# Tile stages of a mixture-of-experts kernel: the first quad in two halves, the second handed over in two, and another order of gate and down products in the first eight quads

## What is computed

```
flat = x.reshape(B * T, D)
logits = flat @ router_w.T + router_bias
scores = softmax(logits); topk_scores, topk_idx = top_k(scores, 4)   # 32 experts
topk_scores = topk_scores / topk_scores.sum(-1)
h = silu(flat @ gate_w[e]) * (flat @ up_w[e]);  expert_out = h @ down_w[e]
out = sum over the 4 chosen experts of expert_out * topk_score
out = out + silu(flat @ sgate_w.T) * (flat @ sup_w.T) @ sdown_w.T     # shared part
```

## Time and profile before

| | us |
|---|---|
| three timed runs | 927.50, 923.75, 927.27 |
| their median | 927.27 |
| the profiled execution, its own time | 923.53 |
| its span (first to last instruction) | 922.3 |
| mean granted TensorE clock | 0.925 of full speed |
| first tile stage, first tile load issued to last POOL scatter issued | 497.15 to 632.87 |
| second tile stage, the same | 765.63 to 899.70 |
| busy in the whole span: PE 82%, PE weight load 67%, DVE 59%, POOL 54%, ACT 46% | |

### The profile page before, as it was taken

The page is one execution under the profiler, slowest core; times in us unless marked ns, Lnnn a source line. Parts: engine busy times, 40 slices in busy tenths (PEclk is TensorE's granted clock), DMA queues, the critical chain, the costliest instruction groups (busy, mean ns, idle before and its releaser), DMA issues.

```text
span 922.3 us, 18791 instructions
## 1 busy us (share of the span) xinstructions
PE 755.3 (82%) x6384; PEld 616.0 (67%) x6384; DVE 546.8 (59%) x1655; ACT 427.9 (46%) x1099; POOL 494.6 (54%) x488
## 2 busy tenths in 40 slices
PE   6899988889999998878998899915988997999600
PEld 5778755579967777767776788813666775888500
DVE  5974585668677758878873444401977662454205
ACT  3567646556145545555521666620454322666500
POOL 5555540016283024655673577776347772677773
PEclk9999979999889999999999999966998999999955
DMA  9999999900050041001112544314101113444216
GB/s 228 220 216 216 215 219 216 209 6 4 4 160 23 1 129 32 2 32 35 48 57 75 136 123 125 102 52 168 43 26 53 55 58 89 122 124 124 72 51 233
DMA packets 125757, 94.67 MB, mean 103 GB/s; under 512 B 10624, under 2 KB 116480, under 8 KB 125664
## 3 DMA queue, kind: packets, MB, share of 16 engines
q1 hardware_dynamic: 113472, 71.19, 33.7%
q0 software_dynamic: 10176, 21.65, 6.8%
q10 hardware_dynamic: 2016, 0.63, 0.3%
HBM read 34.05 MB, written 59.38 MB: 101 GB/s over the span
## 4 chain that ended last, share of the span: by engine, by line
PE 43%; DVE 19%; POOL 19%; issue 11%; ACT 4%; DMA 3%; SPq 0%; POOLq 0%; DVEq 0%; ACTq 0%
POOL expert_rows L677 10%; POOL sorted_rows L445 8%; PE banks L1638 5%; PE banks L1110 4%; PE banks L1685 3%; PE banks L1667 3%; PE banks L783 2%; PE banks L396 2%; PE banks L397 2%; PE banks L398 2%; DVE h L744 2%; PE banks L793 2%; ACT sg L691 2%; PE banks L785 2%; PE banks L784 2%
## 5 line engine op out<-in xcount | busy, mean ns | idle before, releaser
L677 POOL DMA_INDIRECT expert_rows<-y,goal x190 | 182.0, 958 | 92.8 <-issue 53.1
L445 POOL DMA_INDIRECT sorted_rows<-rows_x,row_of x128 | 127.1, 993 | 67.4 <-issue 37.2
L990 ACT ACTIVATE ys<-banks,wtab 128x128 f32<-128x128 f32 x256 | 73.0, 369 | 66.4 <-PE banks L1110 55.9
L744 DVE TENSOR_TENSOR h<-sg,banks 128x512 f32<-128x512 f32 x48 | 33.0, 688 | 97.3 <-ACT sg L691 95.2
L396 PE MATMUL banks<-x_high,w_high 128*128 128x512 f32 x192 | 86.4, 450 | 0.4 <-POOL w_low L880 0.4
L1110 PE MATMUL banks<-w,hT 128*128 128x128 f32 x512 | 73.5, 288 | 13.1 <-DVE hT L1031 12.7
L1110 PEld LDWEIGHTS banks<-w,hT 128*128 128x128 f32 x512 | 66.9, 198 | 21.9 <-DVE hT L1031 19.4
L915 POOL TENSOR_TENSOR x<-ys,x 128x512 f32<-128x512 f32 x44 | 56.2, 1277 | 46.7 <-ACT ys L990 46.2
L398 PE MATMUL banks<-x_high,w_low 128*128 128x512 f32 x192 | 77.8, 405 | 0.0
L397 PE MATMUL banks<-x_low,w_high 128*128 128x512 f32 x192 | 77.5, 404 | 0.0
L204 POOL TENSOR_TENSOR rstd<-rstd,mhalf 128x4 f32<-128x4 f32 x24 | 25.6, 1067 | 82.9 <-DVE rstd L198 82.6
(11 more groups left out here) (300 smaller groups left out, 1899.6 us busy)
## 6 DMA issues: line engine op xcount, KB each, us to landing
sorted_rows<-zeros SPq DMA_DIRECT2D x32, 1120.0 KB, 17.0
tile<-sorted_rows SPq DMA_DIRECT2D x192, 70.0 KB
routed_low<-in_ffn_w SPq DMA_DIRECT2D x8, 512.0 KB, 3.9
w<-in_ffn_w SPq DMA_DIRECT2D x20, 192.0 KB, 3.6
expert_rows<-y,goal POOLq DMA_INDIRECT x190
routed_down<-in_ffn_w SPq DMA_DIRECT2D x8, 256.0 KB, 5.4
sorted_rows<-rows_x,row_of POOLq DMA_INDIRECT x128
xnT<-expert_rows SPq DMA_DIRECT2D x2, 1024.0 KB, 5.6
```

The costliest lines, as they stand in the source:

```text
L445: POOL.indirect_dma_start(sorted_rows, bass.IndirectOffsetOnAxis(self.row_of[:, g, i:i + 1], 0), rows_x[:, 4 * g + i % 4, :], None).then_i ...
L677: POOL.indirect_dma_start(expert_rows, bass.IndirectOffsetOnAxis(goal[:, 4 * q + i:4 * q + i + 1], 0), y[q % 6][:, i * P:(i + 1) * P], Non ...
L990: last = SCL.mul(ys[s % 2][:, j * P:(j + 1) * P], bank[4 + s % 2][:, j * P:(j + 1) * P], wtab[:, t, e:e + 1])
```

## The change

The change touches only the tile stage, and both calls of it.

1. **The wait before quad 0.** `keep_busy(8)` becomes two times two of the same matmuls, with the wait for the last scatter between them; the wait for `shared_added` moves behind quad 0's gate products; the first load of registers moves ahead of it all.
2. **Quad 0 in halves.** Tiles 0 and 1, and tiles 2 and 3, go through all steps on their own: `head_loaded` counts the last two tiles' loads, the halves' transposes go to banks 0 and 1, their h products to banks 6 and 4, their down products to banks 7 and 0. The halved operations of ACT and DVE work on 256 columns instead of 512. `goals` stays whole.
3. **Quads 0 and 1 are handed to POOL in two parts.** POOL issues the first two scatters after the first two weighted copies.
4. **Another order.** For n = 2 and 3 PE computes down(n-1) between the two halves of gate(n); for n = 4 to 7 it does so right behind gate(n), ahead of the transposes of n+1. ACT makes weighted_y(2) ahead of silu(3), and for n = 4 to 7 weighted_y(n-1) between silu(n) and high(n+1). From n = 8 (`LATER`) the order is as before. Three short matmuls (`keep_warm`) fill PE's wait for h of quad 1.

`quad(s, q)` and `left(s, q)` only give the counts that the signals now reach; every engine's work per quad is otherwise unchanged. The diff's core:

```diff
+        head_loaded = signal("head_loaded", 16)
...
+                halves = [slice(0, 2), slice(2, 4)]
+                half_cols = [slice(0, 2 * P), slice(2 * P, GW)]
...
+                def bank_of_rows(q, i):
+
+                    return bank[i // 2 if q == 0 else q % 2][:, i * P:(i + 1) * P]
+
+                def bank_of_hT(q, i):
+                    return bank[4 if q == 0 and i > 1 else 6][:, i * P:(i + 1) * P]
+
+                def bank_of_y(q, i):
+                    return bank[0 if q < 2 and i > 1 else 7][:, i * P:(i + 1) * P]
+
+
+                LATER = 8
...
-                            SP.dma_start(tile[q % 3][:, i, :], sorted_rows[bass.ds(row, P), :]).then_inc(*tile_loaded[q % 3].inc)
+                            SP.dma_start(tile[q % 3][:, i, :], sorted_rows[bass.ds(row, P), :]).then_inc(
+                                *(head_loaded if q == 0 and i > 1 else tile_loaded[q % 3]).inc)
...
-                        POOL.wait_ge(*rows_out_ready(q + 1))
+                        POOL.wait_ge(*left(rows_out_ready, q, 0 if q < 2 else 1))
                         for i in range(tiles_of_quad(q)):
+                            if q < 2 and i == 2:
+                                POOL.wait_ge(*left(rows_out_ready, q))
...
-                    high(0)
-                    for n in range(QUADS):
+                    high_half(0)
+                    high_half(1)
+                    silu_half(0)
+                    silu_half(1)
+                    evict_hT_half(0)
+                    high(1)
+                    evict_hT_half(1)
+                    weighted_y_half(0, 0)
+                    weighted_y_half(0, 1)
+                    silu(1)
+                    high(2)
+                    evict_hT(1)
+                    weighted_y_half(1, 0)
+                    weighted_y_half(1, 1)
+                    for n in range(2, QUADS):
+                        if n == 3:
+                            weighted_y(2)
                         silu(n)
+                        if 3 < n < LATER:
+                            weighted_y(n - 1)
                         if n + 1 < QUADS:
                             high(n + 1)
-                        if n > 1:
+                        if n >= LATER:
                             weighted_y(n - 1)
                         evict_hT(n)
-                        if n == 0:
-                            weighted_y(0)
...
-                    low_t(0)
+                    low_half(0)
+                    low_half(1)
                     goals(0)
-                    for n in range(QUADS):
-                        hidden(n)
-                        if n + 1 < QUADS:
-                            low_t(n + 1)
-                            goals(n + 1)
+                    for n in range(2):
+                        DVE.wait_ge(*silu_ready(n + 1))
+                        hidden(0, halves[n])
+                    for q in range(1, QUADS):
+                        low_t(q)
+                        goals(q)
+                        DVE.wait_ge(*quad(silu_ready, q))
+                        hidden(q)
...
-                    PE.wait_ge(*shared_added(NG))
...
-                    keep_busy(8, bank[5])
...
-                    transposes(0)
-                    for n in range(QUADS):
-                        gate_up_rows(n)
+                    experts_of(0)
+                    keep_busy(2, bank[0])
+                    PE.wait_ge(*dispatched(4 * TOPK * NG))
+                    keep_busy(2, bank[0])
+                    PE.wait_ge(*loaded(0))
+                    transposes(0, range(2))
+                    PE.wait_ge(*head_loaded(2))
+                    transposes(0, range(2, 4))
+                    PE.wait_ge(*t_low_ready(1))
+                    gate_up_rows(0, range(2))
+                    PE.wait_ge(*t_low_ready(2))
+                    gate_up_rows(0, range(2, 4))
+                    PE.wait_ge(*shared_added(NG))
+                    PE.wait_ge(*hr_ready(1))
+                    transposes_h(0, range(2))
+                    PE.wait_ge(*loaded(1))
+                    transposes(1)
+                    PE.wait_ge(*hr_ready(2))
+                    transposes_h(0, range(2, 4))
+                    PE.wait_ge(*hrT_ready(1))
+                    down_rows(0, range(2))
+                    PE.wait_ge(*hrT_ready(2))
+                    down_rows(0, range(2, 4))
+                    PE.wait_ge(*quad(t_low_ready, 1))
+                    gate_up_rows(1, range(2), False)
+                    gate_up_rows(1, range(2, 4))
+                    PE.wait_ge(*loaded(2))
+                    PE.wait_ge(*left(rows_out_ready, 0))
+                    transposes(2)
+                    keep_warm(3, bank[1])
+                    PE.wait_ge(*quad(hr_ready, 1))
+                    transposes_h(1)
+                    for n in range(2, QUADS):
+                        if n % 2 == 0:
+                            experts_of(n)
+                        PE.wait_ge(*quad(t_low_ready, n))
+                        PE.wait_ge(*quad(hr_ready, n - 2))
+                        gate_up_rows(n, range(2), False)
+                        if n > 3:
+                            gate_up_rows(n, range(2, 4))
+                        if n < LATER:
+                            PE.wait_ge(*quad(hrT_ready, n - 1))
+                            PE.wait_ge(*left(rows_out_ready, n - 2))
+                            if n == 2:
+                                down_rows(1, range(2))
+                                down_rows(1, range(2, 4))
+                            else:
+                                down_rows(n - 1)
+                        if n < 4:
+                            gate_up_rows(n, range(2, 4))
                         if n + 1 < QUADS:
+                            PE.wait_ge(*loaded(n + 1))
+                            if n == 3:
+                                PE.wait_ge(*left(rows_out_ready, 1))
                             transposes(n + 1)
-                        if n > 1:
+                        if n >= LATER:
+                            PE.wait_ge(*quad(hrT_ready, n - 1))
+                            PE.wait_ge(*left(rows_out_ready, n - 2))
                             down_rows(n - 1)
+                        PE.wait_ge(*quad(hr_ready, n))
                         transposes_h(n)
-                        if n == 0:
-                            down_rows(0)
...
```

More of the change, by code:

```diff
@@ L655, in sync_engine @@
                         if q > 2:
-                            SP.wait_ge(*tT_mm(q - 2))
+                            SP.wait_ge(*quad(tT_mm, q - 3))
                             SP.wait_ge(*goal_ready(q - 2))
@@ L679, in scalar_engine, with high_half, silu_half @@
                 def scalar_engine():
+                    def high_half(n):
+                        SCL.wait_ge(*tT_mm(n + 1))
+                        SCL.copy(t_high[0][:, half_cols[n]], bank[n][:, half_cols[n]]).then_inc(*t_high_ready.inc)
+                    def silu_half(n):
+                        SCL.wait_ge(*pair_mm(n + 1))
+                        if n == 0:
+                            SCL.wait_ge(*hidden_done(self.steps))
+                        SCL.activation(sg[0][:, half_cols[n]].rearrange("p (i n) -> p i n", n=P), pairs(0)[:, halves[n], 0:P],
+                                       ACT.Silu).then_inc(*silu_ready.inc)
@@ new lines, in evict_hT_half, with weighted_y_half @@
+                    def evict_hT_half(n):
+                        SCL.wait_ge(*hrT_mm(n + 1))
+                        if n == 0:
+                            SCL.wait_ge(*down_done(self.steps))
+                        SCL.copy(hT[0][:, half_cols[n]], bank[(6, 4)[n]][:, half_cols[n]]).then_inc(*hrT_ready.inc)
+                    def weighted_y_half(q, n):
+                        SCL.wait_ge(*goal_ready(q + 1))
+                        SCL.wait_ge(*left(rows_mm, q, n))
+                        for i in range(2 * n, 2 * n + 2):
+                            last = SCL.mul(y[q][:, i * P:(i + 1) * P], bank_of_y(q, i), part[q][:, i, 1:2])
+                        last.then_inc(*rows_out_ready.inc)
@@ L762, in transposes @@
-                    def transposes(q):
-                        PE.wait_ge(*tile_loaded[q % 3](4 * (q // 3) + 4))
-                        if q > 1:
-                            PE.wait_ge(*t_low_ready(q - 1))
-                        for i in range(4):
-                            last = PE.transpose(bank[q % 2][:, i * P:(i + 1) * P], tile[q % 3][:, i, 0:D], ident[:, :])
+                    def transposes(q, those=range(4)):
+                        for i in those:
+                            last = PE.transpose(bank_of_rows(q, i), tile[q % 3][:, i, 0:D], ident[:, :])
@@ L781, in gate_up_rows @@
+                    def gate_up_rows(q, those=range(4), counts=True):
+                        for i in those:
                             ps, rows = pairs(q)[:, i, :], slice(i * P, (i + 1) * P)
@@ L796, in down_rows, with transposes_h @@
```

(16 more changed lines are left out.)

81 lines of the change are left out of this document (42 added, 39 removed).

## The result

The change takes 922.15 us in the median of 20 runs (919.76 to 926.99), before takes 925.83 us (20 runs, 923.04 to 930.35): a ratio of 0.996, with a 95% interval of 0.9944 to 0.9976. That is 3.7 us gained (2.2 to 5.2), with the predicted sign and, at 922.15, inside the predicted range for the time. It is a little over half of the 6.7 us forecast and just under the 4 to 8.5 us given for the gain. At 0.4% it is also less than the 0.5% that the prediction named as what can be told from no change, where it gave a chance of 0.71 to more than that and 0.23 to less; the interval of 20 runs leaves out zero all the same. The profiled execution took 921.16 us (span 919.9) where that of before took 923.53.

A forecast was written before the change was run, and what follows sets the result against it. POOL's scatter issue, 5.05 us a quad, bounds each stage; earlier first issues (5.8, 4.2) plus old holes (1.9, 1.85) less 3.5 gaps each give 6.7 us: 923.53 becomes 916.8, the median 920.5, range 914.5 to 925.

The forecast's parts named there:

- What bounds it: Tile stage: POOL never waits after quad 1, a quad costs it 5.05 us, and its last scatter ends the stage.
- The first issue, second stage: POOL's first scatter issue in the second tile stage comes at 774.94 instead of 779.14, 4.2 us earlier.
- The working by halves: Quad 0 in two halves: step prices from the last tile's landing to POOL's first issue sum to 5.60 us.
- The first issue, first stage: POOL's first scatter issue in the first tile stage comes at 506.46 instead of 512.27, 5.8 us earlier.
- the fourth tile's landing: First stage head: the fourth tile lands at 500.81, three steps of 0.535 and 2.05 us after SP's first issue.
- The supply after it: Quads 1 to 7: the new order leaves POOL gaps of 3.5 us a stage, in place of 1.88 and 1.85.
- The loop: Quads 4 to 6: gate, down, y, copy and rest take 5.12 us a quad, 0.07 over POOL's 5.05.
- The sum: Both tile stages: 4.2 us gained in the first, 2.55 in the second, 6.7 together after rounding.
- moves the end one for one: End of a tile stage: everything after hangs on its last scatter, so time won there shortens the whole equally.
- The gaps don't arise: Rival, after the first issue: POOL runs through without gaps, 7.0 us more gained, 913.5 us; chance 0.10.
- The clock at half in the head: Rival, stage start: PE's clock falls once per stage, up to 1.7 us each, 923.9 us; chance 0.15.
- The clock falls in the loop: Rival, quads 3 to 7: PE's clock falls repeatedly, 2.67 us a turn; slower from four falls each stage; chance 0.06.

The follow-up runs named there:

- the first series: Four follow-up kernels on one chip: old order, prolonged order, new PE start alone in before, long filler in the change; 920.73, 928.99, 930.68, 926.82 us, before 929.78.
- `LATER` = 24: The change with its new order kept to the last quad instead of ending at quad 8; 928.99 us, ratio 0.9993.
- the old order: The change with before's order of PE and ACT put back from quad 2 on; 920.73 us, ratio 0.9899; on two other chips 0.9894 and 0.989.
- the second series: On another chip: the change, the old order, the change without filler, the old order with more filler; 1061.13, 1062.69, 1062.46, 1063.99 us, before 1073.52.
- the third series: Third chip: the change, the old order, new order alone in before, the change with POOL waiting for whole quads; 1065.58, 1067.03, 1078.59, 1069.93 us, before 1077.32.

## Why the prediction was right, and where its size was off

**What bounds it** held on the chip of the prediction: POOL's series is 1.263 us a step in every undisturbed stage, after quad 7 nothing waits, and the stage ends with it.

**The first issue, second stage.** Said 9.31 us after SP's first load, measured 9.36; from the turning of the second half to POOL 5.60 said, 5.72 measured (768.79 to 774.51). The working by halves was right. ACT's halves took 0.37 to 0.38 us, between the 0.41 taken from its own row and the 0.32 that the prediction set beside it, and DVE's 0.42, as said.

**The first issue, first stage.** Said 9.3, measured 9.84. 0.13 of it is again the path (501.97 to 507.70, 5.73). The rest is the term that took the fourth tile's landing from the second stage: PE turned the halves at 500.66 and 501.97, 4.1 us after the first load instead of 3.7.

```profile
497.20 2.84 PE L172 MATMUL banks<-wqkv,ident 128*128 128x384 f32 x8
500.66 0.44 PE L841 MATMUL banks<-ident,tile 128*128 128x128 f32 x2 [0.62 <-DMA tile<-sorted_rows]
501.97 0.44 PE L841 MATMUL banks<-ident,tile 128*128 128x128 f32 x2 [0.87 <-DMA tile<-sorted_rows]
```

**The supply after it.** Said 1.1, 0.6, 1.1, 0.2, 0.5, together 3.5 a stage; measured, less 0.30 each, 1.13, 0.72, 1.12, 0.30, 0.53, together 3.80. The second stage has 4.04 with the pause at 816.45, which no step had. The loop is as it was drawn; from the gate of quad 4 to that of quad 5:

```profile
521.24 0.38 PE L856 MATMUL banks<-routed_high,t_high 128*128 x1 [0.43 <-issue]
...
522.76 1.05 PE L870 MATMUL banks<-routed_down,hT 128*128 x8
...
526.39 0.38 PE L856 MATMUL banks<-routed_high,t_high 128*128 x1 [1.41 <-DVE t_low L800]
```

```profile
523.91 1.14 ACT L760 ACTIVATE y<-banks,part 128x128 f32<-128x128 f32 x4 [0.35 <-PE banks L870]
524.92 0.60 ACT L740 CAST t_high<-banks 128x512 fp32r<-128x512 f32 x1
```

From gate to gate it takes 526.39 - 521.24 = 5.15 us (5.12 said): down waits for nothing, y follows it, the copy follows y, and PE stands 1.41 us.

**The sum.** First stage 4.2 said and 3.36 measured: 0.40 late landing, 0.13 path, 0.30 gaps. Second stage 2.55 and 1.95: 0.05 head, 0.54 gaps, most of it the pause of 0.43. Together 5.3 instead of 6.7. So the largest term that was sized wrong is the gaps, 7.84 over both stages where 7.0 was said; the landing of the fourth tile in the first stage comes next.

The rest of the miss lies outside the stages. The prediction put that at nothing: what is won "moves the end one for one". In the profiled pair it did not. The first stage began 0.71 us later, and 2.17 us were lost between the stages, which leaves 2.4 of the 5.3 us, the difference of the two spans (922.3 and 919.9). The median gain, 3.7 us (2.2 to 5.2), leaves 5.3 just outside as well, so part of that loss is probably in most executions; one pair of profiles can't say how much. How far such times move by themselves the first series shows: SP's first load came at 499.63 to 504.37 us in its four kernels, behind code that none of them changes. In the change the granted clock fell at 672 us (0.63), where before read 1.00. The kernel with `LATER` = 24 also fell there (0.79 and 0.78 from 676 to 684) and also took 134.93 us between its stages; the other three of the first series didn't, and took 132.5 to 134.0. Whether an earlier end of the stage brings this about, or it is chance, stays open.

The forecast time, 920.5, came within 1.7 us of the 922.15 measured partly by luck: the gain was 3.0 us too large, but it was taken off a median of three runs (927.27) that lay 1.4 us above that of twenty (925.83).

**The rivals.** *The gaps don't arise* is refuted by the rows. *The clock at half in the head* did not happen in the change's profile. The same head ran in eight profiled executions, 16 stages over all chips, and its clock fell in one of them, the first of `LATER` = 24, at the cost of 0.84 us behind the turning, half of the 1.7 that the prediction priced. There the second half was turned latest, with 1.19 us idle between the turnings; but the change in the second series had 1.15 us there and kept its clock, so this piece alone doesn't tell the two apart. So the rival's mechanism is real, and rare. *The clock falls in the loop*, given 0.06 and priced at 2.7 us a quad, is real in small: at quad 4, in two of the six undisturbed stages that have the new order, 1.6 us each time, never again and again before the last quads. Both are first stages of the first series in which POOL's first issue came late (11.07 and 11.15 us). In the two stages with the old order it didn't fall there. The rival's count was off: 11.4 us at 2.67 a fall is four to five falls over both stages, not four in each. In no series was the change slower than before, which agrees with the small chance given.

**What the prediction left out** is what the new order is worth by itself. It reckoned the gaps of the new order rightly, one behind the other, and never set them beside the gap that the old order would leave behind the new head. A gap that POOL has before quad n makes room for the quads behind it, so only the latest quad, counted against 5.05 us a quad, sets the end. In before that is quad 1; in the change it is quad 7, where the order turns back behind a loop that runs at 5.15. The old order has quad 1 later (a gap of 2.3 instead of 1.1) and yet ended its stages 1.7 and 1.9 us sooner than the change did in its own measurement, and 2.1 us sooner in the second stage of the same series. So on the undisturbed chips the gain came from the change's other parts, the halves, the hand-over and the shorter filler, and the order took back 1.7 to 2.1 us a stage. On the chip of the third series the head brings the gain too, and on both disturbed chips the order neither gives nor takes what can be measured. How much of the gain the hand-over alone brings stays open, since its test fell on a disturbed chip. The new head with the old order took the least of the four kernels of the first series and was level with the change on the two disturbed chips, so it is a candidate and not a proven winner.

## What to carry to other kernels

Where one engine issues at a fixed pace, write for each unit the time it is ready less its number times the pace: the largest of these sets the end, and moving any other unit earlier buys nothing. An order that saves the first hole must also be cheap where it turns back. And before a filler in front of a matmul stage is cut, ask how long the engine will then stand in one piece. Half the filler was enough where halves of the work came in between (15 of 16 heads kept their clock), but not with whole quads, and no filler was not enough even with halves.

## What the hardware showed beside it

- A filler that looks like 1.2 us of delay was not: with half of it and whole quads, PE idle for 2.1 to 2.3 us and again 1.49 us, the clock fell to 0.5 for about 7 us in the first stage and 10 in the second, by the stretches from 504 and from 776, and the first issue came 0.6 and 2.4 us later than in before, not earlier.
- Where PE stood waiting for it, the second pair of tiles was turned 0.90 to 1.63 us behind the first (872.97 and 873.87 in the change of the second series, 502.50 and 504.13 with `LATER` = 24), with the same four DMAs on SP's queue.
- The highest mean clock did not go with the least time. `LATER` = 24 has 0.947 in the mean and 1.00 to the end of its second stage, and took 928.99 us; the old order has 0.922, falls to 0.50 for the last quads, and took 920.73. There PE has run out of work while POOL still issues, and the fall costs nothing.
- In the first measurement and the first series all medians lie between 920 and 931 us, in the second and third, on two other chips, between 1061 and 1079. There a silu lasts the same 597 ns, but starts up to 7.9 us late, with "remote" or "issue" where a releaser should stand. A change of a few us can't be compared across such chips: before and change must run on the same one.
